# Softmax attentions on two float32r parts of queries and keys, with projections as three float32r products

## The reference

```
# softcap attention: 16 query heads, 8 key/value heads, head size 32
q, k, v = X @ Wq, X @ Wk, X @ Wv
q = q * cos + rotate_half(q) * sin;  k = k * cos + rotate_half(k) * sin
att = q @ k.T * 256 ** -0.5
att = 50 * tanh(att / 50)
y = softmax(causal(att)) @ v @ Wo

# plain attention: 16 query heads, 4 key/value heads, head size 16
q, k, v and the rotation as above
y = softmax(causal(q @ k.T / sqrt(16))) @ v @ Wproj
```

## Time and profile before

| | |
|---|---|
| median of 3 runs | 3083.39 us (3082.63 to 3088.0) |
| the profiled execution | 3089.23 us, span 3087.3 us |
| mean granted clock of TensorE | 0.912 of 2.4 GHz |
| TensorE, VectorE, ScalarE, GpSimd busy | 81%, 68%, 60%, 28% of the span |
| projection `pa`, attention `aa` | 24.6 to 125.8 us, 125.8 to 471 us |
| projection `pb`, attention `ab` | 608 to 667 us, 667 to 1060 us |

### The profile page before, as it was taken

The page is one execution under the profiler, slowest core; times in us unless marked ns, Lnnn a source line. Parts: engine busy times, 40 slices in busy tenths (PEclk is TensorE's granted clock), DMA queues, the critical chain, the costliest instruction groups (busy, mean ns, idle before and its releaser), DMA issues. The chain is left out here.

```text
span 3087.3 us, 69834 instructions
## 1 busy us (share of the span) xinstructions
PE 2494.2 (81%) x25745; PEld 1664.7 (54%) x25832; DVE 2105.2 (68%) x4897; ACT 1849.8 (60%) x3604; POOL 873.3 (28%) x907
## 2 busy tenths in 40 slices
PE   7788877878888698577677677776999686899998
PEld 3333325643343385344444344445888565788888
DVE  7478886668787567599799899985333254666652
ACT  3388874324444443289799799993222332576678
POOL 2233334120000131255455455540000122223223
PEclk9899997878999898799999899998999776898999
DMA  3523312254233212512211222004000565522210
GB/s 123 140 47 66 70 23 91 87 108 56 45 38 42 71 52 98 108 21 29 30 16 14 30 29 29 1 1 169 1 1 1 104 137 96 127 39 33 31 41 11
DMA packets 291483, 174.00 MB, mean 56 GB/s; under 512 B 206416, under 2 KB 252512, under 8 KB 289120
## 3 DMA queue, kind: packets, MB, share of 16 engines
q1 hardware_dynamic: 282000, 161.40, 25.4%
q10 hardware_dynamic: 9168, 8.41, 1.0%
HBM read 113.84 MB, written 51.51 MB: 54 GB/s over the span
## 5 line engine op out<-in xcount | busy, mean ns | idle before, releaser
L1279 ACT ACTIVATE ad_e<-ps,ad_nm 128x1024 f32<-128x1024 f32 (+7 forms) x512 | 384.9, 760 | 96.9 <-DVE ad_nm L1340 94.9
L1340 DVE TENSOR_REDUCE ad_nm<-ps 128x1 f32<-128x1024 f32 (+7 forms) x512 | 369.2, 748 | 54.2 <-PE ps L1210 53.6
L1313 POOL TENSOR_TENSOR ad_e<-ad_e,ad_c 128x128 f32<-128x128 f32 (+7 forms) x256 | 293.6, 1147 | 15.0 <-DVE ad_rz L1353 8.2
L615 ACT ACTIVATE ab_e<-ps 128x512 f32<-128x512 f32 (+3 forms) x384 | 167.6, 490 | 204.7 <-PE ps L532 158.8
L1208 PE MATMUL ps<-ad_k_st,ad_q_st 96*128 96x512 bf16 (+3 forms) x768 | 212.8, 338 | 95.2 <-ACT ad_e L1279 47.1
L365 PE MATMUL ps<-warm,ident_b 128*128 128x512 bf16 x425 | 139.5, 394 | 114.7 <-ACT ad_prT L1264 112.7
L1364 DVE CUSTOM_DVE_ANT_0 ad_t<-ad_e,ad_rz 128x128 f32<-128x128 f32 (+7 forms) x256 | 224.0, 875 | 3.7 <-ACT ad_pr L1287 2.5
L1306 POOL TENSOR_TENSOR ad_e<-ad_e,later_k 128x128 f32<-128x128 f32 x256 | 118.9, 464 | 380.2 <-ACT ad_e L1279 380.2
L1287 ACT ACTIVATE ad_pr<-ad_t,ad_low 128x128 f32<-128x128 f32 (+7 forms) x256 | 201.0, 785 | 0.0
L1223 PE MATMUL ps<-ident,ad_pr 128*128 128x128 f32 x1152 | 174.3, 279 | 23.6 <-ACT ad_pr L1287 23.6
L1825 POOL TENSOR_TENSOR st_it_low<-st_it,st_it_high 128x256 fp32r<-128x256 f32 x128 | 98.3, 780 | 323.8 <-ACT st_it_high L2088 306.9
(11 more groups left out here) (392 smaller groups left out, 7175.0 us busy)
## 6 DMA issues: line engine op xcount, KB each, us to landing
aa_q_st<-scr_a SPq DMA_DIRECT2D x48, 256.0 KB, 5.9
split<-f_split SPq DMA_DIRECT2D x16, 768.0 KB, 3.9
ad_q_st<-scr_d SPq DMA_DIRECT2D x48, 256.0 KB, 9.7
g_w<-split SPq DMA_DIRECT2D x8, 1536.0 KB, 17.9
scr_a<-pa_parts SPq DMA_DIRECT2D x24, 384.0 KB, 2.5
scr_d<-pd_parts SPq DMA_DIRECT2D x20, 384.0 KB, 2.5
st_w_first<-split ACTq DMA_DIRECT2D x5, 1536.0 KB, 7.5
aa_k_st<-scr_a SPq DMA_DIRECT2D x48, 128.0 KB, 6.1
```

Of the source, the lines that this page charges most:

```text
L615: act.activation(e[:, u % ER, h, lo:QB], m.ps[:, n4(u, h) % 3, lo:QB], ACT.Exp, scale=scale).then_inc(s_read[0], 1)
L1279: act.activation(e[:, u % EB, s, 0:L], src, ACT.Exp, bias=nm[:, u % EB, s:s + 1], accum_out=z[:, u % EB, s:s + 1]).then_inc(exped[s], 1)
L1313: pool.tensor_tensor(e[:, k, 1, 0:L], e[:, k, 1, 0:L], c[:, k:k + 1].to_broadcast([P, L]), ALU.mult).then_inc(mixed, 1)
L1340: dve.tensor_reduce(nm[:, u % EB, s:s + 1], src, AX.X, ALU.max, negate=True).then_inc(maxed[s], 1)
```

## The change

Both first-layer attentions use a new projection function, `project_rope_split(..., two=True)`. It calls `norm_transpose` with `high` and `low`, splits the weights on GpSimd into a float32r part and a remainder, in pieces of two tiles, and forms each product as high x high + high x low + low x high in float32r. With `two` the rotated result is stored as two float32r parts instead of three bf16 ones: ScalarE casts, GpSimd subtracts. The two scratch tensors become float32 with two parts instead of bf16 with three. In `attention` the six pairs become three, `Q_TWO` and `K_TWO`: 96 rows in one stack for head size 32, 48 rows for head size 16. The maximum goes in with two rows instead of three. `project_rope` itself gains an unused `two` path, and the differential attention keeps its three bf16 parts.

```diff
@@ project_rope_split: new, called by attn_softcap and attn_plain
+    def split_weights(pool):
+        pool.wait_ge(w_loaded, 32)
+        for n, (lo, hi) in enumerate(pieces):
+            cols = slice(lo * P, hi * P)
+            pool.tensor_copy(w_high[:, :, :, cols], w[:, :, :, cols]).then_inc(w_rounded, 1)
+            pool.wait_ge(w_rounded, n + 1)
+            pool.tensor_tensor(w_low[:, :, :, cols], w[:, :, :, cols], w_high[:, :, :, cols], ALU.subtract).then_inc(w_split, 1)
+        pool.tensor_copy(wv_high[:], wv[:]).then_inc(w_rounded, 1)
+        pool.wait_ge(w_rounded, len(pieces) + 1)
+        pool.tensor_tensor(wv_low[:], wv[:], wv_high[:], ALU.subtract).then_inc(w_split, 1)
+
+    norm_transpose(nc, m, tag + "n", loads=loads, high=x_high, low=x_low, pool_work=split_weights)
...
+    parts = ph.sb("parts", [P, PB, 2, QB], F32R) if two else ph.sb("parts", [P, PB, 3, QB], BF16)
...
+            for n, (mt, tb) in enumerate(items):
+                if tb == 0 and mt % 2 == 0:
+                    pe.wait_ge(w_split, mt // 2 + 1)
+                if n >= 2:
+                    pe.wait_ge(turned, 2 * (n - 1))
+                cols, tok = slice(mt * P, (mt + 1) * P), slice(tb * QB, (tb + 1) * QB)
+                for s in range(2):
+                    out = m.ps[:, 2 * (n % 2) + s, :]
+                    for k in range(KC):
+                        pe.matmul(out, w_high[:, k, s, cols], x_high[:, k, tok], start=(k == 0), stop=False)
+                        pe.matmul(out, w_high[:, k, s, cols], x_low[:, k, tok], start=False, stop=False)
+                        last = pe.matmul(out, w_low[:, k, s, cols], x_high[:, k, tok], start=False, stop=(k == KC - 1))
+                last.then_inc(product, 1)
+            pe.wait_ge(w_split, len(pieces) + 1)
+            for t in range(TILES):
+                if t >= 4:
+                    pe.wait_ge(v_copied, t - 3)
+                out, tok = m.ps[:, 4 + t % 4, 0:kv * hd], slice(t * P, (t + 1) * P)
+                for k in range(KC):
+                    pe.matmul(out, x_high[:, k, tok], wv_high[:, k, :], start=(k == 0), stop=False)
+                    pe.matmul(out, x_high[:, k, tok], wv_low[:, k, :], start=False, stop=False)
+                    last = pe.matmul(out, x_low[:, k, tok], wv_high[:, k, :], start=False, stop=(k == KC - 1))
+                last.then_inc(v_product, 1)
...
+                if two:
+                    pool.wait_ge(high, n + 1)
+                    pool.tensor_tensor(parts[:, n % PB, 1, :], r[:, a, :], parts[:, n % PB, 0, :],
+                                       ALU.subtract).then_inc(low2, 1)
+                    continue
@@ attention
+Q_TWO, K_TWO = (0, 0, 1), (0, 1, 0)
-    stacks = 1 if 6 * hd <= 96 else 2
-    per = 6 // stacks
+    per = len(Q_TWO)
     rows = per * hd
-    aug = 3 if plain else 0
+    aug = 2 if plain else 0
-    q_st = ph.sb("q_st", [rows + aug, 2, HG, stacks, T], BF16)
-    k_st = ph.sb("k_st", [rows + aug, 2, kv_in_group, stacks, T], BF16)
+    q_st = ph.sb("q_st", [rows + aug, 2, HG, T], F32R)
+    k_st = ph.sb("k_st", [rows + aug, 2, kv_in_group, T], F32R)
...
-        q_row = ph.sb("q_row", [rows, 2, HG, T], BF16)
-        k_row = ph.sb("k_row", [rows, 2, T], BF16)
+        q_row = ph.sb("q_row", [rows, 2, HG, T], F32R)
+        k_row = ph.sb("k_row", [rows, 2, T], F32R)
...
             if plain:
                 stage_rows(0)
                 stage_rows(1)
+                sp.wait_ge(ones_set, 1)
...
-                        for st in range(stacks):
-                            last = pe.matmul(m.ps[:, bank, lo:QB], k_st[:, par, h // share, st, kt * P:(kt + 1) * P],
-                                             q_st[:, par, h, st, qb * QB + lo:(qb + 1) * QB],
-                                             start=(st == 0), stop=(st == stacks - 1))
+                        last = pe.matmul(m.ps[:, bank, lo:QB], k_st[:, par, h // share, kt * P:(kt + 1) * P],
+                                         q_st[:, par, h, qb * QB + lo:(qb + 1) * QB], start=True, stop=True)
...
-                dve.tensor_tensor(nmT[:], nmT[:], nmp[:, 0, :], ALU.subtract).then_inc(max_step, 1)
-                step(4)
-                dve.tensor_copy(nmp[:, 1, :], nmT[:]).then_inc(max_step, 1)
-                step(5)
-                dve.tensor_tensor(nmp[:, 2, :], nmT[:], nmp[:, 1, :], ALU.subtract).then_inc(max_step, 1)
+                dve.tensor_tensor(nmp[:, 1, :], nmT[:], nmp[:, 0, :], ALU.subtract).then_inc(max_step, 1)
...
-SCRATCH = {"scr_a": (3, 768, TOK), "scr_b": (3, 384, TOK), "scr_d": (3, 640, TOK)}
+SCRATCH = {"scr_d": (3, 640, TOK)}
```

More of the change, by code:

```diff
@@ L192, in norm_transpose, with project_rope @@
     ph.close()
-def project_rope(nc, m, tag, w_d, tiles, wv_d, kv, hd, vpad, cos_d, sin_d, scr, v_sb):
+def project_rope(nc, m, tag, w_d, tiles, wv_d, kv, hd, vpad, cos_d, sin_d, scr, v_sb, two=False):
     ph = Phase(nc, tag)
@@ L284, in _ @@
                 rotate(n)
-                if n >= 1:
+                if n >= 1 and not two:
                     remainder(n - 1)
                 add(n)
-            remainder(len(items) - 1)
+            if not two:
+                remainder(len(items) - 1)
         @block.gpsimd
@@ L312, in _ @@
                 first_part(n)
-                if n >= 1:
+                if n >= 1 and not two:
                     second_part(n - 1)
-            second_part(len(items) - 1)
+            if not two:
+                second_part(len(items) - 1)
+            if vpad > hd:
+                act.wait_ge(padded, 1)
+            for t in range(TILES):
+                act.wait_ge(v_product, t + 1)
+                act.copy(v_sb[:, t, :, 0:hd],
+                         m.ps[:, 4 + t % 4, 0:kv * hd].rearrange("p (h d) -> p h d", h=kv)).then_inc(v_copied, 1)
@@ L417, in attention @@
     share = HG // kv_in_group
-    N_DMA, SPLIT = 13, 6
+    N_DMA, SPLIT = 2 * per + 1, 4
     PIECES = 12
@@ L445, in stage @@
                 tok = slice(b * T, (b + 1) * T)
-                for n in range(6):
-                    row, st = (n % per) * hd, n // per
-                    sp.dma_start(q_st[row:row + hd, par, :, st, :],
-                                 scr[Q_PARTS[n], j * HG * hd:(j + 1) * HG * hd, tok]
+                for n in range(per):
+                    row = n * hd
+                    sp.dma_start(raw(q_st[row:row + hd, par, :, :]),
+                                 scr[Q_TWO[n], j * HG * hd:(j + 1) * HG * hd, tok]
                                  .rearrange("(h d) t -> d h t", d=hd)).then_inc(staged[par], 16)
                     k0 = q_rows + j * kv_in_group * hd
-                    sp.dma_start(k_st[row:row + hd, par, :, st, :],
-                                 scr[K_PARTS[n], k0:k0 + kv_in_group * hd, tok]
+                    sp.dma_start(raw(k_st[row:row + hd, par, :, :]),
+                                 scr[K_TWO[n], k0:k0 + kv_in_group * hd, tok]
                                  .rearrange("(h d) t -> d h t", d=hd)).then_inc(staged[par], 16)
@@ L461, in stage_rows @@
                 tok = slice(b * T, (b + 1) * T)
[L462 to L464 removed]
+                for n in range(per):
+                    sp.dma_start(raw(q_row[n * hd:(n + 1) * hd, par, :, :]),
+                                 scr[Q_TWO[n], j * HG * hd:(j + 1) * HG * hd, tok]
                                  .rearrange("(h d) t -> d h t", d=hd)).then_inc(row_staged[par], 16)
                     k0 = q_rows + j * hd
[L467 to L468 removed]
+                    sp.dma_start(raw(k_row[n * hd:(n + 1) * hd, par, :]),
+                                 scr[K_TWO[n], k0:k0 + hd, tok]).then_inc(row_staged[par], 16)
             if plain:
@@ L478, in _ @@
                     sp.wait_ge(max_step, SPLIT * (g + 1))
-                    for s in range(3):
-                        sp.dma_start(q_st[rows + s:rows + s + 1, g % 2, :, 0, :], nmp[:, s, :]).then_inc(max_staged, 16)
+                    for s in range(aug):
+                        sp.dma_start(raw(q_st[rows + s:rows + s + 1, g % 2, :, :]), raw(nmp[:, s, :])).then_inc(max_staged, 16)
                     if g + 2 < B * GB:
@@ L495, in run @@
                     if n == 0:
[L496 removed]
+                        pe.wait_ge(row_staged[par], (i + g // 2 + 1) * 2 * per * 16)
                     bank = ROW_BANKS[n4(u, k) % 3]
@@ L643, in _ @@
             if plain:
-                pool.memset(k_st[rows:rows + aug, :, :, :, :], 1.0).then_inc(ones_set, 1)
+                pool.memset(raw(k_st[32:rows + aug, :, :, :]), 1.0).then_inc(ones_set, 1)
                 pool.wait_ge(ones_set, 1)
```

127 lines of the change are left out of this document (113 added, 14 removed).

## The result

The changed kernel takes 3468.52 us (3459.05 to 3470.6, 4 runs) against 3083.72 us before (3082.63 to 3088.0), ratio 1.125, 95% interval 1.122 to 1.1279. I had forecast 3057 us and a range of 3034 to 3079: the sign was wrong, and no rival came near.

The account below looks back on a forecast made before the run. TensorE alone bounds the projections; no engine is full in the attentions. Projections -14 and -5.6, softcap attention -11, plain attention +4 give -26.6 us: 3083.4 to 3057 us, range 3034 to 3079.

Parts of the forecast that it names:

- Does the clock hold?: Softcap attention: TensorE busy 68%, compared with the differential attention at 71% and clock 1.00; so nothing was counted.
- rows don't set the time, columns do: Plain attention: halving the stationary rows saves nothing; each float32r product costs slightly more, 0.228 against 0.217 us at 512 columns.
- rival (d): Plain attention: weight loads show, 91 ns more on 768 matmuls, +70 us, 3127 us in all; chance 0.03.
- +6, ends 0 and +15: Plain attention: extra cost of float32r products for maxima and scores, partly absorbed by TensorE's waits, in us.
- Softcap attention, -10: Softcap attention: fewer ScalarE waits for scores, -10 us, ends 0 and -32.
- Rival (c): Softcap attention: the clock falls; up to 3171 us if low throughout, 3114 us with half low; chance 0.05.
- First products, 29.6 and 17 us: Start of both projections: first product at 29.6 us (softcap), and 17 us after the stage's start (plain), after the splits.
- Items in `pa`: Softcap projection: each pair of output and rotated tiles falls from 3.44 to 2.74 us; 24 items, -16 us taken.
- Values in `pa`: Softcap projection: value products -2.6 us and a lost 2.4 us wait for ScalarE, together -5 us.
- Values in `pb`: Plain projection: value products with 64 columns, between -6 and +6.5 us, -1 taken.
- The start of `ab`: Plain attention: 6 row loads instead of 12 before the first product, same bytes, -2 us.
- The 32 us of maxima: Plain attention's opening stretch at 1.2 GHz: follows VectorE, busy 30.75 of 32 us, so zero change.

Follow-up runs that it names:

- e1: Changed kernel with its plain attention put back to the six bfloat16 pairs of before: 3075.01 us against 3080.88, ratio 0.9977.
- e2: Changed kernel with the plain attention's three float32r pairs staged twice, so 96 and 98 rows: 3099.84 us, one run.
- e3: Kernel before with three of the plain attention's six bfloat16 pairs left out, so 48 and 51 rows: 3351.02 us, one run.
- e8: Changed kernel with 60 bfloat16 products of 128 rows at the start of the plain attention, during its first loads: 3470.27 us, one run.
- the part alone: Kernel before with only the softcap attention changed, its projection multiplying in float32 and storing two float32r parts: 3082.06 us, ratio 1.0001.
- e7: Only the softcap half changed against the kernel before, GpSimd splitting weights at the start of the projection's loop, not during normalisation: ratio 0.9956.
- e9: e7 with one more bfloat16 product of 128 rows ahead of each pair of heads' scores in the softcap attention: 3053.32 us, 0.990 of before.

## Why the prediction was wrong

**The step that failed is "Does the clock hold?"** I put it to the softcap attention alone, and measured it by TensorE's busy share against a row at 71%. The plain attention got no such question, since "nothing is halved" there. But the rows were halved, and "rows don't set the time, columns do" is where the sum went wrong. With 96 rows and more the stage ran at 0.91 in either type, with 48 to 51 at 0.50 to 0.52 in either type (e1, e2, e3), and a warm start does not help (e8). Measured on bfloat16, halving the rows is +269 us where I had zero. The stage was 87% busy before, so there was little slack for any of it.

**The weight loads, rival (d), with 0.03.** My proof that loads overlap was the 0.118 us of the feed-forward's 256-column products, where every neighbour has 128 rows. In the plain attention 512 masks of 128 rows stand between products of 48 and 50, and there the loads do not overlap, which by the estimate above is 118 us of the 269 in bfloat16. The term "+6, ends 0 and +15" measured 25 us at full clock (e2 against e1, staging twice the bytes), more than my upper end and less than the 70 of rival (d), and 122 us at 1.2 GHz and 48 rows. 269 + 122 = 391 is the whole of the stage's +391.5. Taken in the other order, type first and then rows, it is some 28 and 363; either way the rows are the larger part. Whether the clock falls because fewer rows work or because the open loads thin the stream stays open: no run shortened the operand while its loads stayed hidden.

**Softcap attention, -10.** The trace gave -6.4, ten traces some -4 on average, and the part alone nothing that can be measured. Rival (c) was the right mechanism in small: the clock fell from 0.96 to between 0.86 and 0.92 over the stage, and warm products give some 4 us back. My comparison with the row at 71% busy said zero, and the share itself was off: TensorE is busy for 251.19 of 320.1 us, 78%, and not 216 of 318, and the clock fell even so.

**First products, 29.6 and 17 us.** They came at 33.0 and 20.7. The split itself was sized well (GpSimd's piece 1.04 + 2.35 = 3.4 us against 3.25). What I missed is that it runs beside VectorE's scaling and slows it to 2.5 times its duration (e7).

**What held.** Items in `pa`: from 33.04 to the first value product at 100.95 us are 67.9 = 24 x 2.74 + 2.1, the +2 of the cold clock. Values in `pa`: 12.1 us for 17.0, the -5 as forecast. Values in `pb`: 18.6 us against 16.3, +2.3, inside my bounds of -6 and +6.5 but not the -1 that I took; they are 0.11 us apart at full clock and 0.213 at 1.2 GHz, where most of them run. The start of `ab` didn't gain by fewer DMA issues: its first wait is 14.4 us for 13.4. The bytes set it: with as many loads as before but twice the bytes e2 has 22.5 us from the end of `pb`, and with as many as the changed kernel but half the bytes e3 has 9.8. The 32 us of maxima follow VectorE, as said, and that was true of bfloat16 only: in the changed kernel TensorE is busy for 34.29 of 34.30 us there.

The best version of this study is e9: softcap half in float32r, weights split in the loop, warm products, plain half as before: 0.990 and 0.9932 in its two timings.

## What to carry to other kernels

Before a change makes a stationary operand shorter, ask what the clock of that stage will be, and test it with the old type and the new number of rows: here 48 rows in place of 96 halved TensorE's clock while its busy share rose to 98%. A cheaper product is a gain only where its stage needs less TensorE time at the clock that it will then get. A busy TensorE record can hold weight loads: compare the steps from start to start with what the columns need. And a claim that weight loads are hidden holds for the neighbours that it was read from; look whether they have as many rows.

## What the runs showed of the hardware

- The granted clock fell from 1.00 to 0.50 while TensorE's record was busy for 10.00 of 10 us (e8). Part 1 of the Trainium skill's "TensorE: Matmul & The Clock Gate" ties the clock to how busy TensorE has been. These runs neither bear that out nor contradict it, since the records there hold the weight loads.
- With both kinds of products on 96 and 98 rows the plain attention's clock is 0.91, with only the scores on 98 it is 0.55, with neither 0.50.
- A float32r weight load of 128 columns takes 286 to 287 ns (medians) at 1.2 GHz with 48, 50 and 128 rows, a bfloat16 one 104.
- At 1.2 GHz a bfloat16 product of 512 columns and its 128-row mask take 0.53 us with 96 rows and 0.76 with 51; in float32r with 50 rows they take 0.94.
- VectorE's 128x256 scaling took 1019 ns beside GpSimd's float32r split and 408 ns without it.
